# Half-expert interleaving of gathers and scatters, an unread gather, and twelve unread matmuls in a one-core vision tower

## The reference

```python
x_flat = x.reshape(N, Dd)                     # N = 8320, Dd = 128
logits = x_flat @ Wr                          # 8 experts
probs = jax.nn.softmax(logits, axis=0)
vals, idx = jax.lax.top_k(probs.T, C)         # C = 1024 tokens for each expert
selected = x_flat[idx]
h = jax.nn.gelu(jnp.einsum('ecd,edf->ecf', selected, W1) + b1[:, None, :], approximate=False)   # F = 512
out_e = jnp.einsum('ecf,efd->ecd', h, W2) + b2[:, None, :]
weighted = vals[..., None] * out_e
output = jnp.zeros_like(x_flat).at[idx.reshape(-1)].add(weighted.reshape(-1, Dd))
```

## Time and profile before

| | us |
|---|---|
| median of 3 runs | 1003.63 (1002.75 to 1004.59) |
| the profiled execution | 1003.19 |
| its span, from first to last instruction | 1001.4 |
| busy in the span: PE, PEld | 736.4, 393.2 |
| busy: DVE, ACT, POOL | 555.0, 446.7, 473.0 |
| mean granted clock of PE | 0.87 of full speed |

### The profile page before, as it was taken

The page is one execution under the profiler, slowest core; times in us unless marked ns, Lnnn a source line. Parts: engine busy times, 40 slices in busy tenths (PEclk is TensorE's granted clock), DMA queues, the critical chain, the costliest instruction groups (busy, mean ns, idle before and its releaser), DMA issues.

```text
span 1001.4 us, 9698 instructions
## 1 busy us (share of the span) xinstructions
PE 736.4 (74%) x2872; PEld 393.2 (39%) x2872; DVE 555.0 (55%) x1238; ACT 446.7 (45%) x729; POOL 473.0 (47%) x486
## 2 busy tenths in 40 slices
PE   0268589999999999999999986533215599997740
PEld 0123235544544454445445543322215355543310
DVE  0210157778778877787787766773787435311110
ACT  0634356656665666576667433221350233232200
POOL 1233444555455555555455222261100648888775
PEclk9779789999999999999999997866555699998875
DMA  9699998898889888988986120000010223443332
GB/s 218 150 206 208 201 205 197 197 217 196 206 197 217 201 202 195 217 192 203 209 195 161 37 64 21 0 22 10 11 11 4 48 58 62 83 65 64 35 34 24
DMA packets 135647, 126.31 MB, mean 126 GB/s; under 512 B 17588, under 2 KB 125996, under 8 KB 135468
## 3 DMA queue, kind: packets, MB, share of 16 engines
q1 hardware_dynamic: 113600, 91.27, 39.6%
q0 software_dynamic: 19456, 33.44, 17.7%
q10 hardware_dynamic: 2540, 0.99, 0.5%
HBM read 87.92 MB, written 12.98 MB: 101 GB/s over the span
## 4 chain that ended last, share of the span: by engine, by line
PE 26%; DVE 24%; POOL 20%; issue 14%; DMA 8%; ACT 5%; SPq 2%; ACTq 1%; POOLq 0%; DVEq 0%
PE bank L1338 10%; POOL out L617 9%; DMA XS<-in_x 5%; POOL XS L606 5%; DVE Y L955 4%; PE bank L1436 3%; DVE stats L905 3%; DVE O L897 2%; DVE XR L897 2%; DVE QT L1030 2%; ACT XS L812 2%; POOL rsB L489 2%; SPq L418 2%; PE bank L1421 2%; PE bank L1467 2%
## 5 line engine op out<-in xcount | busy, mean ns | idle before, releaser
L1338 PE MATMUL bank<-XS,WT 126*128 126x512 f32 (+1 forms) x608 | 313.6, 651 | 34.8 <-DMA XS<-XS 34.8
L794 ACT ACTIVATE XS<-XS 84x1152 f32<-84x1152 f32 (+1 forms) x192 | 187.9, 1028 | 37.0 <-DMA XS<-in_x 35.7
L1338 PEld LDWEIGHTS bank<-XS,WT 126*128 126x128 f32 (+1 forms) x608 | 112.8, 194 | 170.7 <-issue 170.0
L563 POOL COPY XS<-XS 84x1152 f32<-84x1152 f32 x64 | 89.4, 1397 | 84.1 <-DMA XS<-in_x 80.9
L617 POOL DMA_INDIRECT out<-XS x64 | 100.3, 1567 | 24.6 <-issue 18.6
L606 POOL DMA_INDIRECT XS<-token_rows,XS x64 | 65.0, 1016 | 77.2 <-issue 65.4
L576 POOL DMA_DIRECT2D XS<-XS x128 | 70.6, 554 | 55.5 <-PE bank L1338 40.6
L955 DVE TENSOR_TENSOR_SCAN Y<-qdec,XT 128x512 f32<-128x512 f32 (+1 forms) x68 | 77.4, 1158 | 7.8 <-ACT XT L681 7.8
L837 ACT ACTIVATE XS<-bank,VT 128x512 f32<-128x512 f32 x64 | 44.0, 687 | 66.0 <-PE bank L1544 66.0
L1544 PE MATMUL bank<-XS 128*128 128x512 f32 x128 | 66.4, 667 | 0.8 <-ACT XS L681 0.8
L961 DVE SCALAR_TENSOR_TENSOR ET<-Y,ema_c,ET 128x512 f32<-128x512 f32 (+1 forms) x68 | 61.7, 908 | 1.8
(11 more groups left out here) (229 smaller groups left out, 1282.7 us busy)
## 6 DMA issues: line engine op xcount, KB each, us to landing
XS<-in_x SPq DMA_DIRECT2D x192, 392.0 KB
XS<-XS POOLq DMA_DIRECT2D x128, 189.0 KB, 7.7
out<-O SPq DMA_DIRECT2D x16, 256.0 KB, 6.9
token_rows<-XR SPq DMA_DIRECT2D x16, 256.0 KB, 8.1
XS<-in_L_ffn_W SPq DMA_DIRECT2D x16, 256.0 KB, 3.2
XS<-in_L_tok_W SPq DMA_DIRECT2D x1, 1176.0 KB, 10.3
XS<-token_rows,XS POOLq DMA_INDIRECT x64
out<-XS POOLq DMA_INDIRECT x64, 3.3
```

Source lines behind the costliest of these rows:

```text
L563: pool.tensor_copy(ST[0:ROWS, n % 2, :, :, :].rearrange("p m j r -> p m r j"), px[:, :, :, PASSES:PATCH])\
L794: ins = act.activation(area(slice(0, ROWS), k // 4, piece, m0, m0 + CCOL // 2).rearrange("p m j r -> p m r j"), px[:, :, :, REST * piece:m ...
L1338: ins = pe.matmul(TOK[half][:, :], WT[rows, t, :], area(rows, half, t // REST)[:, :, t % REST, :], start=(t == 0), stop=(t == PASSES - 1))
```

## The change

Five edits, all in the feed-forward part.

1. Gathers and scatters are issued by half-experts. POOL gathers experts 0 and 1, then alternates four scatters of expert e with four gathers of expert e + 2. Each half has its own semaphore, so `rows_in` waits for its own four gathers only; `values` waits for both halves.
2. POOL first issues one gather of row 0 for all partitions (index `zero`) into a buffer that is overwritten later, and waits for it. Nothing reads it.
3. ACT runs a Gelu on one unread column when the search is over, so that the table load comes there.
4. PE issues twelve matmuls whose results nobody reads, identity by the first expert's weights, 512 columns each: one after the counting matmul of the steps 8 to 12 (counted from 0), five after `offsets(0)` and two after `offsets(1)`.
5. On DVE `compares(1)` and `scans(1)` stand before `token_index(0)`, and the one-hots of expert 1 behind `index_lists(0)`; on PE `offsets(1)` stands before `compact(1)`. For the first half the order is its own: `result(0)` comes right behind `rows_in(1)`, ahead of `compact(2)` and `hidden(1)`, and likewise on DVE ahead of the lists of expert 2.

```diff
-        gathered = [count(f"gathered{h}", 16 * 8) for h in range(3)]
+        gathered = [[count(f"gathered{h}{half}", 16 * 4) for half in range(2)] for h in range(3)]
...
-            def gather(e):
+            def gather(e, half):
 
                 h = e % 3
                 pool.wait_ge(*idx_ready.done(e))
@@ -602,18 +606,17 @@
                 if e >= 3:
                     pool.wait_ge(*pe_gt.done(2 * e - 5))
                     pool.wait_ge(*val_r.done(e - 3))
-                for k in range(8):
+                for k in range(4 * half, 4 * half + 4):
                     pool.indirect_dma_start(out=XG[h][:, k, :], out_offset=None, in_=rows_d,
                                             in_offset=bass.IndirectOffsetOnAxis(ap=IDX[:, e, k:k + 1], axis=0))\
-                        .then_inc(gathered[h].sem, 16)
-
-            def scatter(e):
-
-                if e:
+                        .then_inc(gathered[h][half].sem, 16)
+
+            def scatter(e, half):
+
+                if e and half == 0:
                     pool.wait_ge(*scattered.done(e - 1))
-                for k in range(8):
-                    if k % 4 == 0:
-                        pool.wait_ge(*dve_ow.done(2 * e + k // 4))
+                pool.wait_ge(*dve_ow.done(2 * e + half))
+                for k in range(4 * half, 4 * half + 4):
                     pool.indirect_dma_start(out=out_flat, in_=OW[:, e % 2, k, :], in_offset=None,
                                             out_offset=bass.IndirectOffsetOnAxis(ap=IDX[:, e, k:k + 1], axis=0),
                                             compute_op=ALU.add).then_inc(scattered.sem, 16)
@@ -621,13 +624,17 @@
             pool.wait_ge(*row_stored.done(LAST))
             pool.wait_ge(*out_stored.done(LAST))
             pool.wait_ge(*pr_stored.done(0))
-            gather(0)
-            gather(1)
-            gather(2)
+            pool.indirect_dma_start(out=XG[0][:, 0, :], out_offset=None, in_=rows_d,
+                                    in_offset=bass.IndirectOffsetOnAxis(ap=zero, axis=0)).then_inc(primed.sem, 16)
+            pool.wait_ge(*primed.done(0))
+            for e in range(2):
+                for half in range(2):
+                    gather(e, half)
             for e in range(E):
-                if e + 3 < E:
-                    gather(e + 3)
-                scatter(e)
+                for half in range(2):
+                    scatter(e, half)
+                    if e + 2 < E:
+                        gather(e + 2, half)
...
+            act.wait_ge(*cnt_a.done(STEPS - 1))
+            act.activation(seen[0:KEYS, 3, 0:1], seen[0:KEYS, 2, 0:1], ACT.Gelu).then_inc(gelu_ready.sem, 1)
+            act.wait_ge(*gelu_ready.done(0))
 
...
             one_hots(0)
+            compares(1)
+            scans(1)
+            token_index(0)
+            index_lists(0)
             one_hots(1)
-            token_index(0)
-            compares(1)
-            index_lists(0)
-            scans(1)
+            ranks(1)
             token_index(1)
-            ranks(1)
             index_lists(1)
             one_hots(2)
+            values(0)
+            result(0, 0, 0)
+            token_index(2)
+            weigh(0, 0, 0, 0)
+            index_lists(2)
             one_hots(3)
-            values(0)
-            token_index(2)
-            index_lists(2)
-            for n in range(2 * E):
+            for n in range(1, 2 * E):
                 e, half = divmod(n, 2)
-                if n:
+                if n > 1:
                     result(n - 1, 1 - half, (n - 1) // 2)
...
+                if it == 8:
+                    pe.wait_ge(*w_in[0].done(0))
+                if 8 <= it < STEPS - 1:
+                    pe.matmul(bank[6][:, :], ident[:, :], W1s[:, 0, :], start=True, stop=True)
...
-                pe.wait_ge(*gathered[e % 3].done(e // 3))
+                pe.wait_ge(*gathered[e % 3][half].done(e // 3))
...
+            def warm(n):
+
+                for _ in range(n):
+                    pe.matmul(bank[6][:, :], ident[:, :], W1s[:, 0, :], start=True, stop=True)
+
             offsets(0)
+            warm(5)
             compact(0)
             spread_lists(0)
+            offsets(1)
+            warm(2)
             compact(1)
-            offsets(1)
             spread_lists(1)
             rows_in(0, 0, 0)
-            for n in range(2 * E):
+            hidden(0, 0, 0, 0)
+            rows_in(1, 1, 0)
+            result(0, 0, 0)
+            compact(2)
+            rows_out(0, 0)
+            spread_lists(2)
+            for n in range(1, 2 * E):
                 e, half = divmod(n, 2)
                 hidden(n, half, e % 2, e // 2)
-                if n == 0:
-                    compact(2)
-                else:
+                if n > 1:
                     result(n - 1, 1 - half, (n - 1) // 2 % 2)
```

More of the change, by code:

```diff
@@ L1237, in values @@
                 h = e % 2
-                dve.wait_ge(*gathered[e % 3].done(e // 3))
+                for half in range(2):
+                    dve.wait_ge(*gathered[e % 3][half].done(e // 3))
                 if e >= 2:
@@ L1285, in _ @@
                     token_index(e + 3)
[L1286 removed]
+                if not half and e + 2 < E:
                     index_lists(e + 2)
[L1288 removed]
+                if n > 1:
                     weigh(n - 1, 1 - half, (n - 1) // 2 % 2, (n - 1) // 2)
```

9 lines of the change are left out of this document (6 added, 3 removed).

## The result

| | before | after |
|---|---|---|
| median of 4 runs of each, one chip | 1003.48 us (1002.75 to 1004.59) | 988.46 us (987.62 to 991.53) |
| the profiled execution, its span | 1003.19, 1001.4 | 988.4, 986.6 |
| mean granted clock of PE | 0.87 | 0.88 |

The ratio is 0.9863 with a 95% interval of 0.9846 to 0.9881, a gain of 15.0 us. The forecast was 992.6 with a range of 987.5 to 998.0: the direction is right, and the gain lies for the most part in the first gather and POOL's waits, where it was expected; the size is 4 us short. Two views of the changed kernel first, in the columns of the earlier trace rows: the stretches at the end, and what POOL waited for from 760 us.

What follows compares the result with a forecast made beforehand. POOL's queue of gathers and scatters sets the end: first gather, issue work, waits, closing. From 1003.19, -5.8 + 1.4 - 5.9 - 0.7 = -11.0 gives 992.2, on the median 992.6; range 987.5 to 998.0.

Steps and rivals of the forecast that it cites:

- first gather: POOL's first real gather starts 5.76 us earlier, at 767.76: 3.7 from removing its stall, the rest from an earlier index list.
- POOL's waits: POOL's waits for data sum to 10.2 us (4.3, 4.2 and 1.7) in place of 16.1: 5.9 us less.
- POOL's work: POOL's issue work grows by 1.4 us, from more turns between gathers and scatters; the count of real transfers is unchanged.
- the closing: Landing and closing after POOL's last scatter ends: 7.8 us, with no change predicted.
- The rival in which the stall comes back after a long idle time: Before POOL's first real gather: the unread gather does not remove the stall, costing about 0.3 us, 992.9; chance 0.15.
- The search term: Unread matmuls in search steps 8 to 12 may lift TensorE's clock: 0 to 1.5 us gained, 0.7 taken.
- the second wait: At POOL's scatter of expert 0's second half, weighted rows ready at 810.7: a wait of 4.2 us.
- Single scatters cost over 1.6 us: A sign in POOL's scatters that would show the prediction wrong; 1.56 us was usual.
- The clock holding through the small matmuls: Rival on TensorE: POOL's wait of 4.3 shrinks to under 1, the search gives 0.8 more; 988.1; chance 0.16.
- No half ever starved: Rival: a half's path from landing to weighting outgrows POOL's 12.6 us, each of 12 halves waits; about 1011; chance 0.04.
- The unread matmuls were not in the way: Rival before the first compaction: clock does not rise, five take 9 us, the list comes 4 us later; 996.6; chance 0.12.
- no effect: Rival at the end: the transfers themselves, not their issue, set the end; 1003.6; chance 0.05.

Runs made afterwards that it cites:

- the last kernel: Changed kernel with expert 0's second half set ahead on TensorE and VectorE, without three more unread matmuls: 985.35 us, ratio 0.9826 to the kernel before.
- the second and third set: Four kernels each, on chips where the kernel before took 1002.41 and 1002.26 us: 987.89, 990.26, 988.26, 984.69; then 991.04, 997.51, 993.28, 985.35 us.
- the four of the first: Changed kernel without unread gather, without twelve unread matmuls; kernel before with interleaving alone; changed kernel with whole experts: 993.6, 997.07, 1007.47, 1008.47 us; kernel before 1014.12.
- the third set: Changed kernel without twelve unread matmuls 0.9887; kernel before with interleaving alone 0.9951; changed kernel with whole experts 0.991, with expert 0's second half ahead 0.9826.

## Why the prediction was right, and where it was off

Of the 4 us by which the forecast is short, 2.3 lie ahead of the search, for which it had no term. The terms that it had came to 12.5 us for its 11.0, with errors both ways: the first gather with the search (1.0) and POOL's work (1.6) came out worse than predicted, the waits (3.1) and the closing (1.0) better. That the sum came as close as it did is in part luck.

**First gather.** Predicted 5.8 us earlier and another 0.7 from the search; 5.5 from the start of the search on. The list came as worked out (764.72 + 2.32 of shift = 767.04, predicted 767.32). Of the 3.95 us from list to gather I took 3.7 away; 3.2 went, since 0.79 us and not 0.27 are left. The unread gather itself came at 735.97 and not near 730, since the router values land late (last part below); POOL was idle there, so it cost nothing. The page of the Trainium skill named there (GPSIMD Engine Reference, Instruction dispatch) gives about 6 us for the first call of freshly loaded GpSimd code. The traces show 3.9 us, in three kernels; whether the two are the same thing no run here shows. The rival in which the stall comes back after a long idle time is out: POOL stood idle for 28.55 us before the first real gather, which started 0.79 us after its list. By the prediction's own sum the unread gather was worth 0.3 us at the end (992.9 for 992.6), since the first wait would have swallowed the stall; it is worth 2.4 by the medians and 0.6 to 1.7 by the traces. The search term of 0.7 is nothing: the clock stayed at 0.50, and a kernel without those five matmuls is as fast. They took more room than I gave them, too: TensorE idled 0.40 us in a step, for my 0.5 at least, and the steps stayed at 2.79 us.

**POOL's waits.** The term that was off most in size. Predicted 4.3, 4.2 and 1.7; less 0.30 each they are 2.5, 2.9 and 1.8, so the change is -9.0 for -5.9. Where I had the clock low from the second list to the end of the first transposes, the second compaction ran at the high clock (2.07) and the spreading and first transposes too (1.05, 0.66), so PE was ready for the half 1.0 us earlier on the scale of before; POOL meanwhile was through with its gathers 0.9 later than I said. The first hidden layer itself took 6.61 for my 5.81. This wait is no constant: in the second execution of the same kernel the second compaction took 3.65, the hidden layer 5.28, and the wait was 1.47. The second wait was 1.3 us too long in my sum, since the weighed rows came 1.2 earlier (809.52 on the scale of before, for 810.7); what makes it is that expert 1's first half stands ahead of expert 0's second on TensorE and VectorE, as the last kernel shows.

**POOL's work.** Predicted +1.4 for the turns between gathers and scatters, measured +3.0, all of it in scatters: 64 of them take 1614 ns each, 1567 before, and the gathers 65.0 us for 64.9. Four single scatters took 2.00, 2.25, 2.09 and 2.18 us where 1.56 is usual, 2.3 us in excess together. The third, and what VectorE did then:

```profile
849.76 2.09 POOL L620 DMA_INDIRECT out<-XS  x1 [0.30 <-issue]
```

```profile
849.16 1.25 DVE L1226 TENSOR_TENSOR XS<-XS 128x2112 bf16<-128x2112 bf16 x1
850.32 0.76 DVE L1228 TENSOR_SCALAR XS<-XS 128x2112 bf16<-128x2112 bf16 x1
```

And one that lies almost wholly beside one-hots (they start at 790.73) and takes what a first scatter after gathers takes anyway:

```profile
790.64 1.65 POOL L620 DMA_INDIRECT out<-XS  x1 [2.76 <-DVE XS L1270]
```

All four of the long ones lie beside one-hots, and so does every scatter over 1.8 us in the 14 traces, 49 of them. But being beside them is not enough: 13 scatters of the changed kernel overlap one-hots, and the other nine took 1.55 to 1.65 us. What decides it was not found. In the kernel before only three scatters overlap one-hots, and none takes over 1.8 us; by interleaving more of them come to lie there. I had looked at this effect for gathers and not for scatters. "Single scatters cost over 1.6 us" stood in my list of what would prove me wrong, and of this term it did. The page of the Trainium skill that I had named there (DMA: Bandwidth & Descriptors, SWDGE vs HWDGE vs iDMA) says that VectorE locks GpSimd, in VectorE's two-port modes, out of the state into which it writes descriptors. The trace agrees in so far as four scatters beside one-hots took 0.4 to 0.7 us more; that the one-hots run in such a mode no run here shows.

**Left out.** The closing is 1.0 us shorter (6.82 for 7.83). It goes with the interleaving: 6.75 to 6.94 in every trace that has it, 7.79 and 7.86 with whole experts. Why was not found; I had put it at no change. The other 2.3 us lie ahead of the search, in code that no edit touches. They are there by about 155 us into the execution. In the eight traces of the second and third set the 128x520 operation starts between 705.71 and 707.83 (706.98 with the interleaving alone), in the four of the first between 706.74 and 709.02; the one trace of the kernel before has 708.84. I don't know whether that is chance or whether other code shifts it; the median's 15.0 us against 12.5 for the terms behind the search leaves room for both.

**The rivals.** The clock holding through the small matmuls (988.1) gives the measured time nearly (its terms add up to 4.7 us and not to 4.5, so 987.9), but that is chance. A piece of it happened, the spreading and the first transposes at the higher clock (1.05 and 0.66); its largest term did not, since the clock fell to 0.50 before the first hidden layer (6.61 us, not 3.5), and the search gave nothing. No half ever starved: between the second wait and expert 7's scatter no transfer of POOL waits over 0.31 us. The unread matmuls were not in the way (2.09 for the compaction). A gain of 15 us rules out no effect.

**What each part is worth**, by ratios of the second and third set: leaving out the unread gather costs 2.1 thousandths, the twelve unread matmuls 2.7, the interleaving 5.0, of 14.0 in all. Each of these ratios has an interval of about 2 thousandths to either side, and the last two compare two chips, so the order of size is shown and the tenths are not. The rest, about 4 us, belongs to parts I did not take out alone (the new orders on VectorE and TensorE, the earlier Gelu), for which the third set gives some 4 us together, and to what the parts take from one another, which was not measured. The Gelu table load, 1.28 us, now lies at 749.42 behind the last count; it was not tested.

## What to carry to other kernels

When one engine's queue sets the end, write the end as first start, plus issue work, plus waits, plus closing, and fill it in for both traces: each edit then shows in one term, and an edit that only moves the first start is partly eaten by the next wait for data. Unread matmuls paid where they stood right before the matmuls they were to speed up, and did nothing in the search. The first compaction took 2.09 us in all nine traces that have the five ahead of it, and 3.65 in all five without them. The second, with two ahead, took 2.07 to 2.16 in five of those nine traces and 3.65 in four. Neither group was taken out alone. Look at which half the next transfer in the queue belongs to, and finish that half first; and put experiments of under 1% beside the kernel they are compared with on the same chip, since four ratios to the kernel before taken elsewhere were off by 1.6 to 7.2 thousandths.

## What the runs showed of the hardware that I had not expected

- TensorE's clock stayed at 0.50 for the search's last five steps with PE idle for only 0.40 of each 2.79 us, and rose within 6.87 us of gapless matmuls behind it.
- The clock fell to 0.50 at about 765.4 while TensorE was working, and with no idle time over 0.89 us since its rise near 758.6; what ran in between were the last unread matmuls and small ones of 64, 8 and 6 columns.
- The same kernel's clock changes place from one execution to the next: the second compaction took 2.07 and 3.65 us in two executions, the first hidden layer 6.61 and 5.28, and GpSimd's first scatter started at +84.12 and +82.78. The second compaction in the second execution:

```profile
768.92 3.65 PE L1535 MATMUL bank<-XS 128*32 128x64 bf16 x65 [0.88 <-DVE XS L1229]
```

- GpSimd pays a stall of 3.9 us ahead of its first indirect transfer, and ahead of no later one in these traces. The unread gather waits for the router values, whose store is issued at 724.13 and takes 7.9 us to land (the next two fences, SyncE's timeline and the DMA issues), and starts at 735.97, 3.94 us after that; the real gather some 30 us later starts 0.79 us after its list.

```profile
724.13 0.63 SPq L465 DMA_DIRECT2D token_rows<-XS  x1
```

```profile
token_rows<-XS SPq DMA_DIRECT2D x1, 260.0 KB, 7.9
```

- Some scatters issued beside VectorE's one-hots take 2.0 to 2.25 us for 1.56 in the changed kernel's first trace, and up to 2.89 in others (the first one with the interleaving alone); others beside them take 1.55 to 1.65.
- One chip ran the kernel before in 1014.12 us, others in 1002.3 to 1003.5, and the four kernels traced on it show pauses on TensorE or VectorE inside this part.
